# Cross attention: the older quad's weighted sum is taken ahead of the scores, not behind them

## The reference, cut to what matters

```python
q = (query @ Wq.T + bq).reshape(b, lq, HEADS, HEAD_DIM)      # 16 heads of 32
k = (key @ Wk.T + bk).reshape(b, lk, HEADS, HEAD_DIM)        # key = value = ctx, 722 rows
v = (value @ Wv.T + bv).reshape(b, lk, HEADS, HEAD_DIM)
scores = jnp.einsum('bqhd,bkhd->bhqk', q * scale, k)
probs = jax.nn.softmax(scores, axis=-1)
attn = jnp.einsum('bhqk,bkhd->bqhd', probs, v).reshape(b, lq, HIDDEN)
```

## Time and profile before

| what | us |
|---|---|
| timed runs | 2443.78, 2445.39, 2446.67 |
| median | 2445.39 |
| profiled execution, span from the first to the last instruction | 2446.1 |
| TensorE busy in the span | 2364.8 |
| VectorE / ScalarE / GpSimd busy | 1536.4 / 1329.7 / 1360.7 |

### The profile page before, as it was taken

The page is one execution under the profiler, slowest core; times in us unless marked ns, Lnnn a source line. Parts: engine busy times, 40 slices in busy tenths (PEclk is TensorE's granted clock), DMA queues, the critical chain, the costliest instruction groups (busy, mean ns, idle before and its releaser), DMA issues.

```text
span 2446.1 us, 58715 instructions
## 1 busy us (share of the span) xinstructions
PE 2364.8 (97%) x21644; PEld 2051.2 (84%) x21644; DVE 1536.4 (63%) x2621; ACT 1329.7 (54%) x3301; POOL 1360.7 (56%) x1189
## 2 busy tenths in 40 slices
PE   7999968989999999999999999999999899999999
PEld 7888847888888888888888888888888698998998
DVE  6666677845667767667767676767676825435342
ACT  5777762115666666666666666666666651221311
POOL 5676563326666666657667566666665532333332
PEclk9999978999999999999999999999999999999999
DMA  7687776635677677677677677776777841101010
GB/s 224 190 226 193 191 200 244 235 119 152 186 199 198 194 193 196 187 204 198 183 196 199 189 207 195 184 204 189 191 196 202 231 130 65 40 26 64 0 39 23
DMA packets 293198, 408.91 MB, mean 167 GB/s; under 512 B 148540, under 2 KB 168508, under 8 KB 292924
## 3 DMA queue, kind: packets, MB, share of 16 engines
q1 hardware_dynamic: 268348, 354.96, 51.3%
q10 hardware_dynamic: 24576, 50.36, 8.1%
HBM read 138.81 MB, written 52.43 MB: 78 GB/s over the span
## 4 chain that ended last, share of the span: by engine, by line
PE 73%; DVE 1%; SPq 1%; DMA 1%; issue 1%; POOL 0%; ACT 0%; ACTq 0%; POOLq 0%; DVEq 0%
PE D_ps_p L68 41%; PE D_ps_s L1873 7%; PE D_ps_p L1900 6%; PE E_ps_g L68 6%; PE E_ps_u L68 6%; PE E_ps_d L68 5%; PE E_ps_y L68 3%; SPq L1293 1%; PE E_ps_t L1926 0%; DMA E_x_last<-x 0%; DVE D_columns L1677 0%; DMA D_pT<-D_turned 0%; DVE D_turned L1691 0%; DMA E_w_int<-in_w_gate 0%; ACT D_e L1542 0%
## 5 line engine op out<-in xcount | busy, mean ns | idle before, releaser
L1405 POOL TENSOR_SCALAR D_e<-D_e,D_columns 128x722 f32<-128x722 f32 x256 | 538.5, 2104 | 468.5 <-DVE D_columns L1683 468.5
L1542 ACT ACTIVATE D_e<-D_ps_s,D_columns 128x723 f32<-128x723 f32 x512 | 437.8, 861 | 391.7 <-DVE D_columns L1677 347.2
L1677 DVE TENSOR_REDUCE D_columns<-D_ps_s 128x1 f32<-128x723 f32 x512 | 439.6, 899 | 295.4 <-PE D_ps_s L1873 295.2
L1691 DVE STREAM_TRANSPOSE D_turned<-D_e 128x768 f32<-128x768 f32 x512 | 496.1, 973 | 18.8 <-DMA D_pT<-D_turned 17.0
L68 PE MATMUL D_ps_p<-D_ctx_high,cross_wk_high 128*128 128x362 f32 (+1 forms) x1024 | 350.1, 342 | 2.5 <-DVEq L1703 1.5
L68 PE MATMUL D_ps_p<-D_ctx_low,cross_wk_high 128*128 128x362 f32 (+1 forms) x1024 | 336.7, 329 | 0.0
L68 PE MATMUL D_ps_p<-D_ctx_high,cross_wk_low 128*128 128x362 f32 (+1 forms) x1024 | 334.9, 327 | 0.0
L68 PE MATMUL D_ps_p<-cross_wv_high,D_ctx_high 128*128 128x512 f32 (+1 forms) x656 | 259.8, 396 | 0.0
L68 PE MATMUL D_ps_p<-cross_wv_high,D_ctx_low 128*128 128x512 f32 (+1 forms) x656 | 259.3, 395 | 0.0
L68 PE MATMUL D_ps_p<-cross_wv_low,D_ctx_high 128*128 128x512 f32 (+1 forms) x656 | 257.7, 393 | 0.0
L1549 ACT ACTIVATE D_e<-D_e,D_columns 128x722 f32<-128x722 f32 x256 | 231.0, 902 | 9.2 <-DVE D_columns L1683 9.2
(11 more groups left out here) (230 smaller groups left out, 5274.8 us busy)
## 6 DMA issues: line engine op xcount, KB each, us to landing
D_pT<-D_turned SPq DMA_DIRECT2D x1536, 96.0 KB, 2.6
D_pT<-D_turned ACTq DMA_DIRECT2D x512, 96.0 KB, 2.7
D_craw<-in_ctxT SPq DMA_DIRECT2D x124, 361.0 KB, 4.1
self_q<-A_q_out SPq DMA_DIRECT2D x10, 640.0 KB, 4.1
self_k<-A_k_out SPq DMA_DIRECT2D x10, 640.0 KB, 3.9
self_v<-A_v_out SPq DMA_DIRECT2D x25, 256.0 KB, 3.6
A_q<-self_q SPq DMA_DIRECT2D x32, 200.0 KB, 3.6
A_k<-self_k SPq DMA_DIRECT2D x32, 200.0 KB, 4.4
```

What stands on the lines that cost most here:

```text
L1405: pool.tensor_scalar(head, head, inv[:, 2 * (s % 2):2 * (s % 2) + 1], None, ALU.mult)\
L1542: act.activation(e[n // 2 % 2][:, n % 2, 0:PARTS * PART].rearrange("p (a c) -> p a c", a=PARTS), parts_of(n), ACT.Exp, bias=neg_max[:, n % ...
L1677: dve.tensor_reduce(neg_max[:, n % 4:n % 4 + 1], parts_of(n), AX.XY, ALU.max, negate=True)\
L1691: dve.transpose(turned[quad % 2][:, :, 2 * (s % 2) + h, :].rearrange("p j (t r) -> p t j r", r=32), e[s % 2][:, h, :].rearrange("p (t j r) ...
```

## The change

At an even step TensorE takes the weighted sum of the quad three pairs older first, and the scores behind it. Nothing else changes: the same instructions with the same waits, the same list of banks, the same orders on the other engines and queues.

```diff
                 for s in range(FIRST, MAIN + 1):
+                    if s in sum_at:
+                        weighted_sum(sum_at[s])
                     if 0 <= s < STEPS and s % 2 == 0:
                         scores(s // 2)
-                    if s in sum_at:
-                        weighted_sum(sum_at[s])
                     for kind, b, n in unit_at.get(s, []):
```

## The result

The changed kernel takes 2536.07 us (median of four runs, 2532.35 to 2538.87) against 2446.03 us for the kernel before beside it: ratio 1.0362, 95% interval 1.0345 to 1.0379. It is 90 us slower. The forecast was slower, at 2528. The profiled execution of the changed kernel took 2532.35 us with a span of 2530.6, so the two profiled spans differ by 84.5 us, and that is the number which the traces must account for. The rest of the 90 is spread between executions: the profiled one of the changed kernel is the fastest of its four, 3.7 us under their median.

What follows compares the result with a forecast made beforehand. TensorE's own stream, busy 97% of the span, was taken to bound the kernel. 70 us in short pairs, 6 in long pairs and 5.5 at the ends made 82 us, hence 2528 us, range 2512 to 2545.

Steps and rivals of the forecast that it cites:

- The stream itself: TensorE's work per pair: nothing added or removed, the same costs of changing matmul kinds in another order, 0 us.
- Rival (b): On TensorE, scores behind a sum start later than keys do: 18 us more, 2546 us; chance 7 in 100.
- Step 1: In short pairs the sum waits for ScalarE's copy of the odd step's keys: 1.05 us each, 70 us.
- the prediction's chain: Short pairs: scores, VectorE's maxima and sum's copy, odd maxima, ScalarE's exponentials, then copy of keys ending 9.34 us behind scores.
- Long pairs escape step 1: In long pairs the keys' copy ends at about 10.4 us, before the sum is due at 11.18: 0 us.
- one sign in the profile: VectorE's waits for scores in the profile after were to grow by about 70 us.
- Step 2: Unit behind the even step's keys waits for VectorE's copy of the sum: 0.12 us, 6 us over long pairs.
- The ends: Pairs 2, 124 and 125: sums held by copies delay the next scores by 1.6, 1 and 2.8 us, together 5.5.
- rival (c): TensorE's clock falls through idling in short pairs, long pairs take 5% more: 33 us, 2561 us; chance 3 in 100.
- Probabilities by DMA: Sums come earlier against their probabilities' DMAs, but with 6 us of slack in a tight case: 0 us.
- The sum: Total over the whole kernel: 70 + 6 + 5.5 = 82 us on the span of 2446.1, hence 2528 us.

Runs made afterwards that it cites:

- experiment 10: New order except at the loop's last step, with the sum's copy, both steps' key copies and the odd step's values copy moved earlier: 2451.28 us, ratio 1.0014.
- experiment 2: Changed kernel with VectorE copying the sum out of its bank ahead of the two maxima at even steps: 2527.49 us, ratio 1.0327.
- experiment 1: Changed kernel with ScalarE copying the odd step's keys ahead of its two exponentials: 2477.60 us, ratio 1.0119.
- experiment 4: Kernel before (old order) with the odd step's keys copied ahead of ScalarE's exponentials: 2448.88 us, ratio 1.0004.
- experiment 6: Changed kernel with the sum ahead of the scores only behind a pair of three units, old order elsewhere: 2471.16 us, ratio 1.0093.
- experiment 7: Changed kernel with ScalarE copying the odd step's keys one operation later, behind the scaling of its head: 2705.12 us, ratio 1.1060.
- experiment 8: Kernel before (old order) with the odd step's keys copied late, behind ScalarE's scaling of its head: 2450.88 us, ratio 1.0018.
- experiment 3: Changed kernel with odd keys copied ahead of the exponentials and the sum copied ahead of the maxima: 2468.87 us, ratio 1.0079.
- experiment 5: Changed kernel with the old order, scores ahead of the sum, at the loop's last step only: 2529.38 us, ratio 1.0336.

## Why the prediction was right

**The stream itself: 0.** Right, and shown by experiment 10. Rival (b) put up to 18 us on scores behind a sum; they start 1.19 behind it (1250.90 to 1252.09), and keys had started 1.18 behind it.

**Step 1: 70 us in short pairs.** Measured 72.7. The reckoned pair was 9.34 + 0.11 + 1.18 = 10.63, the measured mean is 10.669 (median 10.66). Each link can be seen in the short pair above: the copy ends 9.34 behind the scores, as it did in the other order, and the sum's first weights load 0.11 later (1250.87). 67 sums were expected to be held for 0.7 us each, 50 in all; in the stretch of these pairs 67 waits took 53.4 us. One link of the prediction's chain was wrong and did no harm. It put the sum's copy on VectorE between the scores and the copy of keys; experiment 2 moved that copy ahead and the pair kept its length, so the path goes through ScalarE's exponentials beside it. Experiments 1, 2, 4, 6, 7 and 8 show the copy as the cause, its place on ScalarE as the size, and the length of TensorE's stream since the scores as the condition.

**Long pairs escape step 1.** Right. The reason given was that the copy of the even step's values would no longer come late: ScalarE waits 0.29 us for them in the pair above, where it had waited 1.33, and the keys' copy ends 10.45 behind the scores (10.4 predicted). The same thing made one sign in the profile larger than I said. VectorE's waits for scores were to grow by about 70 us and grew by 129: beside the 81 us that the pairs grew, its waits for exponentials shrank by 38 us (from 103.0 to 64.8) and those for DMAs before a transpose by 14 (from 17.0 to 3.1), and together these come to 133. I take it that this time passed into the wait for scores; no run separates it.

**Step 2: 0.12 us, 6 us in long pairs.** Measured 8.1, or 0.15 a pair. Experiment 2 took it away (12.379). That it vanishes in short pairs is right too, and so does the third wait of experiment 3, which I had missed; it made no difference to the time here, and 15 us (67 x 0.22) once steps 1 and 2 were gone (experiment 3).

**The ends: 5.5 us.** Pair 2 cost 1.6, as predicted. Pair 124 cost 0.8 (1 predicted). Pair 125 was to take 13.06 and took 14.20, and pair 126 grew by 2.1, to which I had given nothing: this is rival (c)'s clock, at one place. I had set the clock aside because TensorE stays busy 93% of a short pair, which held (1.00 in the steady part), but had not asked it of the one long idle stretch at the end. The sum and the scores behind it took 0.98 and 1.29 us more than at full rate, 2.3 of the 3.0 us by which pairs 124 to 126 went over the forecast (6.8 against 3.8).

**Probabilities by DMA: 0.** Right: one wait of 0.4 us, before a sum's weight load. The room is not endless, as the one wait of 2.02 us in experiment 1 shows.

**The sum.** 82 predicted on the span, 84.5 measured. That they lie so close is partly luck, for the parts ahead of pair 2 and behind the last scores happened to be 3.6 and 1.2 us shorter in the profiled execution. The steps by themselves gave 72.7 + 8.1 + 1.6 + 6.8 = 89.2, near the 90 of the medians, so the forecast was 3 us short in step 1, 2 in step 2 and 3 at the ends. All three errors have one sign: each term was taken from one pair read closely, at full clock. The mean pair was a little worse, and at the end the clock fell. What stays open is the spread of 0.02 to 0.04 us a pair in steps 1 and 2; I didn't look further.

## What to carry to other kernels

Two kinds of work that share a rotation of two banks are bound by whoever copies the banks out; before moving one of them, measure from the head of the softmax chain both when its bank's copy ends and when the engine will ask for it, since the difference is the cost and it repeats in every turn. An engine 97% busy can lose to a wait that the profile before doesn't show at all, because the old order covered it. And a wait taken away uncovers the next in the list of banks: here four copies had to move before the stream ran unbroken.

## What the runs showed of the hardware

TensorE's clock fell behind idle stretches of 2.02 us (experiment 7), 2.97 us (experiment 5) and 4.79 us (the changed kernel), and not behind 67 stretches of 0.8 us with a granted clock of 1.00 around them. The 1.77 us of the kernel before, in front of the scores of quad 126, left them at 1.50 us.

The length of the stretch alone doesn't decide. In experiment 7 the clock fell in 42 of 68 places with 1.8 us or more and not in the other 26, though 62 of the 68 were within 0.03 us of 2.00 us. In experiment 10 the scores of quad 126 waited 2.94 us, almost as long as in experiment 5 at the same step, and ran at full rate behind it:

```profile
1917.42 1.50 PE L1883 MATMUL D_ps_s<-D_keys,D_queries 32*128 32x241 f32 x24 [2.94 <-ACT D_e L1542]
```

What decides is not shown here.

The price is not in the wait but behind it: scores of 2.79 instead of 1.50 us in all three. Where it falls varies. In the place shown for experiment 7 the sum right behind the idle stretch still took 1.39 us, near full rate, and only the scores after it ran at half; in the changed kernel the sum was slow too, at 2.23 us.

The Trainium skill (TensorE: Matmul & The Clock Gate, Part 1) says that the gate passes either half of the clock pulses or all of them, by recent activity. The traces agree: the granted clock was 0.52 over the slow sum and scores of the changed kernel, and 0.50 over the slow scores of experiment 5 (from 1997.5 to 2000.5 us).
